# A two-block transformer and graph kernel: attention turned to one tile per batch item, 32x32 score matmuls, exponential behind the transposes, keys masked by GpSimd

## What is computed

```python
# layer 0
cmod = silu(c) @ w_ada + b_ada        # six vectors of shift, scale and gate per item
k, q, v = split(modulate(ln(x)) @ w_qkv)
w = softmax((q / 8) @ k.T)            # per item and head, 32 x 32
x = x + gate * ((w @ v) @ w_proj + b_proj)
x = x + gate * (gelu(modulate(ln(x)) @ w_mlp1 + b_mlp1) @ w_mlp2 + b_mlp2)
# layer 1
self_feat = concat(x, c or 0) @ W_self.T + b_self
for d in (0, 1):                      # adjacency, and its transpose; 11 labels per edge
    aff = (q_d @ k_d.T) / sqrt(8)     # keys: the first 20 tokens
    aff = where(sum_of_labels > 0, aff, -9e15) + labels @ w_bias + b_bias
    out += (softmax(aff) @ self_feat[:, :20]) @ Wout[d, head] + bout[d]
return x + relu(self_feat + out)
```

## Time and profile before

| | |
|---|---|
| median of three runs | 135.92 us |
| span of the profiled execution | 137.4 us |
| busy: PE, DVE, ACT, POOL | 102.6, 92.2, 80.1, 56.6 us |
| mean granted TensorE clock | 0.898 of full speed |

### The profile page before, as it was taken

The page is one execution under the profiler, slowest core; times in us unless marked ns, Lnnn a source line. Parts: engine busy times, 40 slices in busy tenths (PEclk is TensorE's granted clock), DMA queues, the critical chain, the costliest instruction groups (busy, mean ns, idle before and its releaser), DMA issues.

```text
span 137.4 us, 3252 instructions
## 1 busy us (share of the span) xinstructions
PE 102.6 (75%) x1238; PEld 76.3 (56%) x1238; DVE 92.2 (67%) x224; ACT 80.1 (58%) x196; POOL 56.6 (41%) x70
## 2 busy tenths in 40 slices
PE   0396899269968580485899989799699697699651
PEld 0383778169946430231444456678498596598540
DVE  5797995941986899816444088789875748426880
ACT  3009679966595150033032889969959969837511
POOL 7269999999991699102000001222422322402000
PEclk9999999955999959559999999999999999856985
DMA  4996000000000000334000000000000000000004
GB/s 133 423 417 258 0 2 0 0 7 0 5 0 5 0 0 0 34 97 110 0 0 5 0 0 0 0 0 5 2 5 2 5 0 5 0 0 5 5 4 148
DMA packets 4543, 5.78 MB, mean 42 GB/s; under 512 B 2480, under 2 KB 3632, under 8 KB 4272
## 3 DMA queue, kind: packets, MB, share of 16 engines
q1 hardware_dynamic: 4096, 4.52, 9.8%
q10 hardware_dynamic: 432, 1.05, 2.0%
HBM read 4.88 MB, written 0.69 MB: 41 GB/s over the span
## 4 chain that ended last, share of the span: by engine, by line
PE 37%; ACT 23%; DVE 22%; issue 11%; DMA 2%; POOL 2%; ACTq 0%; DVEq 0%; POOLq 0%
ACT Vz L635 11%; PE ps_t L578 7%; PE ps_s L568 6%; PE ps_d L520 5%; PE ps_d L524 5%; DVE masked L766 4%; PE ps_d L459 4%; DVE xn_tok L709 4%; PE ps_y L589 4%; ACT PT L681 3%; ACT E L676 3%; ACT Kz L624 3%; DVE stats L698 3%; DMA x_tok<-in_x_tok 2%; PE ps_d L536 1%
## 5 line engine op out<-in xcount | busy, mean ns | idle before, releaser
L450 POOL TENSOR_TENSOR E<-E,neg_max 128x320 f32<-128x320 f32 x15 | 10.9, 726 | 49.9 <-DVE neg_max L884 49.9
L568 PEld LDWEIGHTS ps_s<-Kz,Qm 128*128 128x128 f32 x192 | 26.6, 213 | 2.2 <-issue 1.4
L568 PE MATMUL ps_s<-Kz,Qm 128*128 128x80 f32 (+1 forms) x192 | 27.7, 294 | 0.1
L635 ACT ACTIVATE Vz<-ps_d 20x128 f32<-20x128 f32 (+1 forms) x96 | 25.7, 267 | 2.3 <-PE ps_d L497 1.1
L578 PE MATMUL ps_t<-ident,E 128*128 128x128 f32 x96 | 16.8, 303 | 6.7 <-ACT PT L681 5.1
L681 ACT ACTIVATE PT<-ps_t 128x512 f32<-128x512 f32 x24 | 14.3, 596 | 12.8 <-PE ps_t L578 12.6
L645 ACT ACTIVATE hidden<-ps_d,cols 128x512 f32<-128x512 f32 x8 | 5.4, 686 | 19.8 <-PE ps_d L520 19.8
L578 PEld LDWEIGHTS ps_t<-ident,E 128*128 128x128 f32 x96 | 11.5, 154 | 9.0 <-ACT E L676 5.7
L589 PE MATMUL ps_y<-Vz,PT 128*32 128x36 f32 x768 | 12.0, 210 | 4.4 <-ACT Vz L635 1.8
L589 PEld LDWEIGHTS ps_y<-Vz,PT 128*32 128x32 f32 x768 | 9.3, 120 | 8.3 <-ACT PT L681 3.8
L520 PE MATMUL ps_d<-xm,w_rest_sb 128*128 128x512 f32 x16 | 9.5, 724 | 5.7 <-DVE xm L718 5.2
(11 more groups left out here) (96 smaller groups left out, 188.8 us busy)
## 6 DMA issues: line engine op xcount, KB each, us to landing
Qm<-in_adj SPq DMA_DIRECT2D x1, 1408.0 KB, 8.4
w_rest_sb<-in_w_rest SPq DMA_DIRECT2D x1, 1088.0 KB, 10.6
bias_rep<-bias_dram SPq DMA_DIRECT2D x4, 160.0 KB, 3.0
x_tok<-in_x_tok ACTq DMA_DIRECT2D x2, 256.0 KB, 3.6
xT<-in_xT ACTq DMA_DIRECT2D x1, 512.0 KB, 5.4
w_ada_sb<-in_w_ada SPq DMA_DIRECT2D x1, 384.0 KB, 4.3
out<-x_tok SPq DMA_DIRECT2D x1, 256.0 KB, 2.3
w_qkv_sb<-in_w_qkv SPq DMA_DIRECT2D x1, 192.0 KB, 5.6
```

The costliest lines, as they stand in the source:

```text
L450: pool.tensor_tensor(e, e, nm.unsqueeze(2).broadcast_to([P, UB * HQ, M]), ALU.add)\
L568: ins = pe.matmul(ps_s[i % 2][:, b * P:b * P + HQ * nk], Qm[d][:, g * UB + b, :, :], Kz[d][:, g * UB + b, :, 0:nk], start=True, stop=True)
L635: ins = act.activation(Vz[d][QUAD * hq:QUAD * hq + nk, h * BH + b:(h + 1) * BH:UB, :, hq * C:(hq + 1) * C], src[:, :, hq, :, :], ACT.Copy)
```

## The change

The unit is turned. Rows of a score tile are now the 128 tokens of four items, columns are heads and keys, so that the exponential, the bias, the reciprocals and the output are all in token order.

- Scores: 16 matmuls of a 32-row, 32-column stationary operand (the queries of one item in one quadrant of features, unmasked) with `Kb`, in which the keys stand four times with another head masked in. Quadrant j writes bank j, item b writes partitions 32b: 32 instructions a unit for 8. `ps_s` is now four banks and single; `ps_y` is single; `ps_d` has two banks.
- q is read once (`q0T`, `q1T`), k four times. In layer 1 ACT copies k once into `k_raw`, and POOL writes the four masked copies (step `keys`, before the scores).
- The transposes read the shifted scores, and ACT's exponential reads `ps_t` and writes `PT` (L671): one ACT pass a unit for two. The pad columns of `E1` hold -30000.
- V is made in column tiles: four matmuls of 32 output partitions per item, for layer 1 both directions at once and only for 20 keys; each evacuation takes 512 columns (L655).
- Layer 1's bias needs no layout of heads: `bias_rep` and its eight DMAs are gone, DVE adds `bias_dir` directly. The label sums are 33 POOL instructions on a label-major adjacency that is read as integers, and the mask is POOL's too.
- The end: selfT with the output biases (`selfb`) and x2 are transposed to token order ahead of it (`sbtok`, `x2tok`); POOL adds selfb to direction 0 (`ya`), DVE adds direction 1 and applies relu and residual group by group; nothing is transposed behind the last unit.
- `ORDER` is written anew, now with every DVE and POOL step of its own, and the banks of dense products are listed.

```diff
-    ("scores", 8), ("soft", (8, None)), ("sub", 8),
+    ("dense", ("mlp1", 1, 3)), ("scores", 8), ("badd", 8), ("dense", ("k1", 0, 1)), ("take", (("mlp1", 1, 3), 0)),
...
+POOL_KEYS = [(0, 0), (0, 1), (1, 0), (1, 1)]
...
+                elif stage == "keys":
...
+                    for q in range(HI):
+                        ins = pool.tensor_scalar(Kb1[d][:, h * BH:(h + 1) * BH, q, :], k_raw[:, d, :, :],
+                                                 cols[:, R_K + d:R_K + d + 1], head_mask[:, 1, q:q + 1],
+                                                 ALU.add, ALU.mult)
+                    ins.then_inc(keys_ready, 1)
...
-                    if i >= 2:
-                        pe.wait_ge(*((scores_read, i - 1 - N0) if UNITS[i - 2][0] else shift_of(i - 2)))
+                    if i >= 1:
+                        pe.wait_ge(scores_read, i)
                     nk = M if layer else S
+                    qT, Kb = (q1T[d], Kb1[d]) if layer else (q0T, Kb0)
                     for b in range(UB):
-                        ins = pe.matmul(ps_s[i % 2][:, b * P:b * P + HQ * nk], Qm[d][:, g * UB + b, :, :],
-                                        Kz[d][:, g * UB + b, :, 0:nk], start=True, stop=True)
+                        for j in range(HJ):
+                            q = slice(QUAD * j, QUAD * j + QUAD)
+                            ins = pe.matmul(ps_s[QUAD * b:QUAD * b + QUAD, j, 0:HI * nk], qT[q, g * UB + b, :],
+                                            Kb[q, g * UB + b, :, :], start=True, stop=True)
...
-                    if i >= 2:
-                        pe.wait_ge(y_ready, i - 1)
+                    if i >= 1:
+                        pe.wait_ge(y_ready, i)
...
-                    act.activation(E[:, i % 3, :, 0:nk], E[:, i % 3, :, 0:nk], ACT.Exp).then_inc(exp_ready, 1)
-                elif stage == "copy":
...
-                    act.activation(PT[:, i % 2, :, :], ps_t[:, :].rearrange("p (b t) -> p b t", t=P), ACT.Copy)\
+                    act.activation(PT[:, i % 2, :, :], ps_t[:, :].rearrange("p (j t) -> p j t", t=P), ACT.Exp)\
```

More of the change, by code:

```diff
@@ L464, in dense_product @@
                 k = DENSE.index(name)
-                if k >= len(ps_d):
-                    wait_taken(pe, DENSE[k - len(ps_d)])
+                earlier = [m for m in DENSE[:k] if BANKS[m] == BANKS[name]]
+                if earlier:
+                    wait_taken(pe, earlier[-1])
                 kind, h = (name, 0) if isinstance(name, str) else name[0:2]
-                if kind in ("xnT", "q", "k"):
+                if kind in ("xnT", "q", "k", "v"):
                     g0, g1 = STARTS[h]
@@ L580, in _ @@
+                    for j in range(HJ):
+                        ins = pe.transpose(ps_t[:, j * P:(j + 1) * P], E[:, i % 3, j * HI:(j + 1) * HI, :], ident[:, :])
                     ins.then_inc(turned, 1)
@@ new lines, in take_part @@
+                if kind == "k":
+                    return dve.tensor_scalar(Kb0[:, bs, part, :], ps_bs, head_mask[:, 0, part:part + 1], None, ALU.mult)
+                if kind == "v":
+                    dve.wait_ge(vz_ready[0], 1)
+                    q = slice(QUAD * part, QUAD * part + QUAD)
+                    return dve.tensor_copy(Vz[q, bs, 0, :, part * C:(part + 1) * C],
+                                           ps[q, :].rearrange("p (b j c) -> p b j c", j=HJ, c=C))
+                if kind in ("proj", "mlp2"):
+                    dve.wait_ge(taken_dve, DVE_TAKES.index((("cmod", 1), 0)) + 1)
+                    bias, gate = (R_PROJ, 2) if kind == "proj" else (R_MLP2, 5)
+                    return dve.scalar_tensor_tensor(out=gated[:, bs, :], in0=ps_bs, scalar=cols[:, bias:bias + 1],
+                                                    in1=over_s(cmod, gate, bs), op0=ALU.add, op1=ALU.mult)
@@ new lines, in take_part @@
+                if kind == "self":
+                    dve.wait_ge(taken_dve, DVE_TAKES.index((("rowsum", h), 0)) + 1)
+                    return dve.scalar_tensor_tensor(out=selfT[:, bs, :], in0=ps_bs, scalar=cols[:, R_SELF:R_SELF + 1],
+                                                    in1=zeroed_q[:, :, :], op0=ALU.add, op1=ALU.add)
+                if kind == "q1":
+                    d = name[2]
+                    return dve.tensor_scalar(q1T[d][:, bs, :], ps_bs, cols[:, R_Q + d:R_Q + d + 1], None, ALU.add)
```

941 lines of the change are left out of this document (464 added, 477 removed), and 22 rows, old and new, of tables (BANKS, ORDER, UNITS).

## The result

The changed kernel takes 124.44 us (median of four runs, 123.29 to 125.86); the kernel before took 137.45 beside it. The ratio is 0.907 (95% interval 0.903 to 0.912): faster by 9%, half of the gain forecast. The profiled execution has a span of 123.5 us. Both kernels' times differ from one execution to the next (135.6 to 139.4 us before, 119.9 to 125.9 over eight of the changed kernel) with the mean clock that PE gets, both profiles above are of slower ones, the ratios compare the faster ones, and where runs differ by less than 3 us the stretches are compared too.

A forecast was written before the change was run, and what follows sets the result against it. No engine was taken as full; PE, at 86% in layer 1's attention, as nearest to a bound. Five stretches (17.1, 27.5, 19.9, 43.5, 4.0) summed to a span of 112 us, times 0.989 gives 111; range 104 to 125.

The forecast's parts named there:

- The sizes of the new operations: Prices of new instructions: score unit 0.5 us in layer 1, 0.7 in layer 0; POOL pass of 320 columns 0.75 to 0.95.
- PE's 86%: PE's busy share in the old second attention stretch, taken as the filling reached in both attention stretches of the new kernel.
- layer 1's attention: Stretch 4: PE work of 37.3 us at 86% filling needs 43.5 us, ending at 108.
- layer 0's attention: Stretch 2, first maximum to first mlp1: DVE work of 23.5 us at 86% filling takes 27.5 us, to 44.6; before 41.7.
- Step 3: First mlp1 to the scores of layer 1: 19.9 us, to 64.5; before 26.2.
- Its cover holds: In stretch 3, PE's three mlp1 and q1 fill its 3.4 us wait for the masked key copies.
- Step 1: Start to first maximum: 17.1 us, 2 more than before, with two memsets holding DVE's normalization until 12.4.
- The end: Behind the last values: reciprocal, product, sum and relu, 4.0 us in place of 6.8, ending at 112.
- From span to time: Whole kernel: forecast span of 112 us times 0.989, the old median over the old profiled span, gives 111 us.
- GpSimd: Rival: GpSimd is late, at 1.6 us a tensor_scalar in labels and keys; 118 us, chance 0.12.
- The clock rival: Small tiles may not hold PE's clock up; half clock a third of stretches 2 and 4: +15, 126 us; clock or drain 0.13.
- drain: Each change of tile shape on PE drains it, 0.2 us at 48 changes, 9.6 in all: 121 us; clock or drain 0.13.

The follow-up runs named there:

- e4: Changed kernel plus 512 value-shaped matmuls (2048 PE instructions, 8 blocks) behind PE's last values; 149.68 us.
- e2: Changed kernel with V products made four items at a time as before the change, 960 PE instructions fewer, V's output layout left out; 116.12 us, ratio 0.859.
- e5: The changed kernel unaltered, run again as the measure for the runs beside it; 122.95 us, profiled span 121.5.
- e1: Changed kernel with GpSimd's two Vz memsets waiting until the first two groups are normalized; 121.82 us, ratio 0.897 to the kernel before.
- e10: Changed kernel plus four unread 256-column matmuls in PE's waits late in layer 0, to keep its clock up; 122.52 us, ratio 0.891 to the kernel before.
- e8: Changed kernel with V made four items at a time and PT and Vz in bfloat16, 1728 PE instructions fewer; 110.98 us, ratio 0.813 to the kernel before.

## Why the prediction was wrong

- *The sizes of the new operations: right.* A score unit of layer 1 takes 0.35 to 0.43 us (0.5 taken), and tiles of 32x32 do run side by side. A POOL pass was too dear in the sum: 0.61 us for the keys (0.75 to 0.95 taken), and 0.48 to 0.78 for the labels (0.8 to 0.9 taken). Three groups of the changed kernel:

```profile
L569 PE MATMUL ps_s<-Kb,q1T 32*32 32x80 f32 x512 | 7.6, 245 | 1.6 <-issue 1.6
L435 POOL TENSOR_SCALAR Kb<-k_raw,cols,head_mask 128x320 f32<-128x320 f32 x16 | 9.6, 613 | 7.9 <-ACT k_raw L647 7.9
L413 POOL TENSOR_TENSOR label_bias<-label_bias,label_tmp 128x256 f32<-128x256 f32 x10 | 7.7, 773 | 0.0
```

- *The step that failed: "I take PE's 86% of the earlier trace rows as the filling that such a list reaches", with a sum in which the delivery of PE's instructions costs nothing.* The 86% was read from a program with 2476 PE instructions and carried over to one with 4556, with each burst priced at its issue rate (32 MATMULs in 0.40 us). The change adds 12 score matmuls a unit (24 x 12 x 4 = 1152 instructions) and 232 V matmuls (928), 8 blocks in all, and no term of the sum and no rival had them. The runs showed that PE gets a block each 3.69 us when it uses them up at once (e4), and that the kernel is 6.5 us faster by the ratios without 240 of its matmuls (e2), 4.3 of it in layer 1's attention, where PE had only 1.5 us less work at the same clock.
- *What that is in layer 0's attention (3.6 us too little).* DVE had the work that was summed (23.2 us for 23.5) and filled 75% of the stretch, not 86%. In e2 it fills 86% (23.1 of 26.9 us). 1.5 us of the 3.6 are the clock (31.1 us in the first profile, 29.6 in e5); the gap of 2.4 us is in both (2.2 in e5).
- *And in layer 1's attention (3.8 us too little).* Here 86% came out by luck, of other terms: PE has 40.7 us of work for 37.3 and fills 86% of 47.3 us. 1.2 us of the 3.4 are the clock and cost nothing: e1 and e10, at 1.00, are no shorter (47.2 and 47.1). The other 2.2 us are missing in PE's sum. The products of k, q and v, taken at 7.9 us, show 10.5 in the table by line; which of them was priced too low isn't worked out. With fewer instructions the list fills more than 86%: 89% in e2 (42.8 us) and 92% in e8 (38.3 us). So two errors of opposite sign stand behind the 86%: the list can fill more than that, and the gaps of 5.3 us, which no term had, take it back.
- *Step 3 (first mlp1 to the scores of layer 1), 3.5 us too little.* 1.4 of it is the clock, shown by e10. The other 2 us are in PE's own list, read from the timelines (of e10 for the full clock) and not tested: at full clock it is 8.45 us from the first mlp1 to mlp2 (7.5 taken, which left out the two value units and the transposes between), and the scores wait in the end for two mlp1 products (70.91 to 72.83 us in the changed kernel), not for the keys, which POOL has ready at 71.92. "Its cover holds" was the wrong way round by about 1 us.
- *Step 1, 1.2 us too little.* The memsets held the normalization, as was said (3.98 and 3.97 us), and e1 shows that to be 3.3 us of the start. They ended sooner than taken (11.8 us for 12.4); what was too small is the way from there to the first maximum, 6.4 us from the normalization's end (11.93) for 4.7. In the timeline q and k take 2.05 us on PE for 0.9, and four transposes (1.30 us) and the V product ahead of the scores (1.08 us) are in no term. This was read, not tested.
- *The end, 0.6 us too much.* One sum and one relu behind the last product, as was said.
- *From span to time.* 0.989 divides the median of before (135.92) by the span of another execution than the median one, whose own time, by the following, was about 139.3. In one and the same execution the time is 1.8 to 1.9 us above the span (125.33 for 123.5, 121.75 for 119.9), so the forecast span of 112 is a time of 113.9, and 111 holds only if the new kernel varies with the clock as the one before did. The stretches are compared by spans, 123.5 for 112, and this doesn't touch them.
- *The rivals.* GpSimd is not late. The clock rival gave 121 to 126, and the time lies in it, but for another reason: the clock costs some 1.4 us in the third stretch, 1.5 and more in layer 0 and nothing that shows in layer 1's attention, not 15. No drain is seen where scores follow values: 128x32 and 32x32 tiles follow each other at the 0.40 us that the first group takes to issue (changed kernel, timeline):

```profile
30.14 0.47 PE L595 MATMUL ps_y<-Vz,PT 128*32 128x36 f32 x32
30.54 0.52 PE L569 MATMUL ps_s<-Kb,q0T 32*32 32x128 f32 x32
```

  The range (104 to 125) held the time by its upper end only.

## What to carry to other kernels

Count the instructions of an engine, not only its busy time: when small tiles replace large ones, several blocks of 256 MATMULs and weight loads in a row took PE about 3.7 us each here (single packets came as little as 3.4 us apart, and one block by itself ran faster, 128 MATMULs in 1.30 us). A gap without a releaser inside a group that waits for nothing is the sign of it. A float32 matmul is four such instructions and a bfloat16 one two, so precision also buys supply. Where POOL has a long memset to do, put it behind a semaphore of the DVE work that it would hold: here that was 3.3 us of the start, though the times show only 1.4 us of it.
